# Moving the second half's LayerNorm from the boundary between two token halves into the first half's expert loop

## The reference

```python
mod = (silu(c) @ wmod).reshape(B, 6, 1, D)     # sa, ca, ga, sb, cb, gb
h = layernorm(x) * (1 + ca) + sa
x = x + ga * attn(h)                            # causal attention, then @ wo
h = layernorm(x) * (1 + cb) + sb
# ffn(h):
shared = (silu(h @ Wsg) * (h @ Wsu)) @ Wsd
probs = softmax(h @ W_g); combine = probs kept at its top 2
y_e = (silu(h @ W_gate[e]) * (h @ W_up[e])) @ W_down[e]   # all 8 experts, all tokens
x = x + gb * (shared + sum_e combine[:, e] * y_e)
```

## Time and profile before

| | |
|---|---|
| median of 3 runs | 1937.34 us (1935.97 to 1938.6) |
| profiled execution, its own time | 1932.17 us |
| its span, core 2 (all cores 1918.4 to 1930.2) | 1930.2 us |
| mean granted TensorE clock, core 2 | 0.787 |
| busy: TensorE matmul, VectorE, ScalarE, GpSimd | 67%, 39%, 22%, 11% |
| chain that ended last: TensorE, VectorE, issue, DMA, ScalarE | 57%, 16%, 11%, 8%, 7% |
| first down matmul of expert 0 for tiles 8 to 15 | at 1536.14 us |

### The profile page before, as it was taken

How to read it: one execution, slowest core, us unless ns; L and a number is a source line. 1 busy time by engine, 2 the same in 40 slices (tenths; PEclk the granted TensorE clock), 3 DMA queues, 4 the chain that set the end, 5 groups by cost and what they waited for, 6 DMA issues and landing times.

```text
span 1930.2 us, 20470 instructions; the slowest of 8 cores (1918.4 to 1930.2 us)
## 1 busy us (share of the span) xinstructions
PE 1288.8 (67%) x5238; PEld 487.1 (25%) x5238; DVE 755.2 (39%) x1449; ACT 434.2 (22%) x735; POOL 216.1 (11%) x226
## 2 busy tenths in 40 slices
PE   3713263236767431658979889799914599999998
PEld 0111121110221101222323333243302233333333
DVE  0354534551144515354233323444354433333333
ACT  0030201210046243415434335310132100000010
POOL 0002020033455773000000000000000000000000
PEclk8955556558965655667989899899956799999999
DMA  9605150079987674000111011021210021121225
GB/s 284 165 0 163 46 164 1 25 228 313 287 247 226 212 213 167 1 1 26 63 44 66 23 44 66 22 66 66 66 43 1 22 66 66 66 66 66 67 78 184
DMA packets 90437, 193.99 MB, mean 101 GB/s; under 512 B 14184, under 2 KB 14248, under 8 KB 90328
## 3 DMA queue, kind: packets, MB, share of 16 engines
q1 hardware_dynamic: 64848, 130.64, 22.4%
q10 hardware_dynamic: 16648, 33.60, 5.8%
q0 software_dynamic: 8832, 28.45, 3.7%
HBM read 155.92 MB, written 36.70 MB: 100 GB/s over the span
## 4 chain that ended last, share of the span: by engine, by line
PE 57%; DVE 16%; issue 11%; DMA 8%; ACT 7%; DVEq 1%; ACTq 0%; POOL 0%; SPq 0%; POOLq 0%
PE ps L950 13%; PE ps L917 13%; PE ps L932 12%; DMA stage<-wmod 5%; PE ps L1088 4%; PE ps L552 4%; PE ps L453 3%; PE ps L1031 3%; DVE h1b L545 2%; DVE h1b L542 2%; DVE st_sm L505 2%; DMA q_aug<-bbf 2%; PE ps L706 2%; PE ps L607 1%; ACT pT L1093 1%
## 5 line engine op out<-in xcount | busy, mean ns | idle before, releaser
L950 PE MATMUL ps<-down_bf,act_e 128*128 128x512 bf16 x1152 | 292.2, 392 | 38.2 <-DVE act_e L940 15.4
L917 PE MATMUL ps<-hT,gate_bf 128*128 128x512 bf16 x1152 | 283.4, 391 | 20.5 <-ACT r_t L886 13.7
L932 PE MATMUL ps<-hT,up_bf 128*128 128x512 bf16 x1152 | 274.4, 381 | 2.0 <-ACT r_t L886 0.8
L940 DVE TENSOR_TENSOR act_e<-ps,silu_s 128x512 bf16<-128x512 f32 x144 | 99.6, 691 | 422.9 <-PE ps L932 353.4
L959 DVE SCALAR_TENSOR_TENSOR x_res<-ps,comb,x_res 128x512 f32<-128x512 f32 x256 | 192.1, 750 | 145.4 <-PE ps L950 141.6
L552 PE MATMUL ps<-ident,h1b 128*128 128x128 f32 x256 | 69.2, 425 | 268.7 <-DVE h1b L545 268.7
L926 ACT ACTIVATE silu_s<-ps 128x512 bf16<-128x512 f32 x144 | 86.0, 597 | 554.1 <-PE ps L917 553.9
L1093 ACT ACTIVATE pT<-ps 128x512 bf16<-128x512 f32 (+3 forms) x320 | 158.8, 531 | 140.2 <-PE ps L1088 127.8
L950 PEld LDWEIGHTS ps<-down_bf,act_e 128*128 128x128 bf16 x1152 | 99.8, 99 | 225.3 <-issue 149.3
L917 PEld LDWEIGHTS ps<-hT,gate_bf 128*128 128x128 bf16 x1152 | 112.8, 100 | 167.8 <-issue 45.1
L932 PEld LDWEIGHTS ps<-hT,up_bf 128*128 128x128 bf16 x1152 | 112.9, 98 | 143.1 <-issue 11.2
(11 more groups left out here) (118 smaller groups left out, 842.7 us busy)
## 6 DMA issues: line engine op xcount, KB each, us to landing
stage<-wmod ACTq DMA_DIRECT2D x96, 256.0 KB, 10.3
gate_bf<-wc_g SPq DMA_DIRECT2D x72, 256.0 KB, 4.8
up_bf<-wc_u SPq DMA_DIRECT2D x72, 256.0 KB, 3.4
down_bf<-wc_d SPq DMA_DIRECT2D x72, 256.0 KB, 3.6
pc_in<-w_gate SPq DMA_DIRECT2D x64, 256.0 KB, 6.1
pc_in<-w_up SPq DMA_DIRECT2D x64, 256.0 KB, 4.2
pc_in<-w_down SPq DMA_DIRECT2D x32, 512.0 KB, 4.2
wc_g<-pc_o POOLq DMA_DIRECT2D x36, 256.0 KB, 4.9
```

Source lines behind the costliest of these rows:

```text
L917: tok = P.op("t", lambda e, buf=buf, hc=hc, qc=qc, dc=dc, psg=psg: e.matmul(psg[:, :], gate_bf[:, buf, dc, 128 * hc:128 * (hc + 1)], hT[:, ...
L932: tok = P.op("t", lambda e, hc=hc, qc=qc, dc=dc, psu=psu: e.matmul(psu[:, :], up_bf[:, dc, 128 * hc:128 * (hc + 1)], hT[:, dc, 512 * qc:51 ...
L940: P.op("v", lambda e, hc=hc, qc=qc, ssl=ssl, psu=psu: e.tensor_tensor(act_e[:, hc, 512 * qc:512 * (qc + 1)], psu[:, :], silu_s[:, ssl, :], ...
L950: tok = P.op("t", lambda e, i=i, dch=dch, hc=hc, psd=psd: e.matmul(psd[:, :], act_e[:, hc, 128 * i:128 * (i + 1)], down_bf[:, hc, 512 * dc ...
```

## The change

The LayerNorm of tiles 8 to 15 and its eight routers become a function, `emit_ln2h2`. The loop of the first half's mixture calls it once, as a whole, after the first unit at which the attention steps are through and all eight `attn_out_tile` have been emitted; if that never happened, it is called behind the loop. Its callback has only the routers. Expert 0's gate and up for tiles 8 to 15 are no longer in the callback but are ordinary units of the second half's list (`skip_e0_gateup=False`). `gate_dma(0, ...)` and `up_dma(0)` keep their place behind the loop and now come after the LayerNorm's instructions in the text.

```diff
+        ln2h2_done = [False]
+
+        def emit_ln2h2():
+            ln2h2_done[0] = True
+
+            def _grp_cb1(grp):
+                for i in range(8 + 4 * grp, 8 + 4 * grp + 4):
+                    emit_router(i)
+
+            layernorm_phase(t0=8, ngrp=2, group_cb=_grp_cb1, pstb=(2, 3),
+                            dump=stage[:, 0:2, :].rearrange("p a b -> p (a b)"),
+                            dump_bufs=[b_stage[0], b_stage[1]])
+
         units = moe_unit_list(0, skip_e0_gateup=True)
...
                 _fin2()
                 if ui % 3 == 0:
                     attn_out_tile(ao_left.pop(0))
+            elif st_done >= nst and not ln2h2_done[0]:
+                emit_ln2h2()
...
-        h2buf = _gbuf[0]
-        gate_dma(0, h2buf)
+        if not ln2h2_done[0]:
+            emit_ln2h2()
+        gate_dma(0, _gbuf[0])
         up_dma(0)
-
-        def _grp_cb1(grp):
-            for i in range(8 + 4 * grp, 8 + 4 * grp + 4):
-                emit_router(i)
-            emit_gateup(0, h2buf, 2 + grp)
-
-        layernorm_phase(t0=8, ngrp=2, group_cb=_grp_cb1, pstb=(2, 3),
-                        dump=stage[:, 0:2, :].rearrange("p a b -> p (a b)"),
-                        dump_bufs=[b_stage[0], b_stage[1]])
-        for u in moe_unit_list(1, skip_e0_gateup=True):
+        for u in moe_unit_list(1, skip_e0_gateup=False):
             u()
```

## The result

The changed kernel is **slower by 0.46%**: ratio 1.0046, 95% interval 1.0031 to 1.0061, medians 1945.62 against 1937.13 us over 11 runs each. The forecast was 1944.7 and slower.

A forecast was written before the change was run, and what follows sets the result against it. A VectorE and ScalarE chain was taken to set the pace inside the 134.8 us around the norm, TensorE outside. Terms summed to +7.4 us, 1939.6 by the profiled execution, carried over to 1944.7 us; range 1940.5 to 1950.0.

The forecast's parts named there:

- Where the code lands: The whole LayerNorm with its routers is emitted after expert 7's third down tile, 57.3 us earlier; TensorE's hole moves along.
- (a): Callback of group 0: without gate and up, 26.91 us becomes the router chain's 16.3, -10.6 us.
- (b): Norm of group 1: with no matmuls ahead, its first transposes run slow too, +0.4 us.
- (c): Callback of group 1: 27.81 us becomes 16.1, a router chain less one table load plus 1.0 before tile 4, -11.7 us.
- (d): Expert 7's remaining down tiles 4 to 7: 10.1 us becomes 10.3 with a partly cold start, +0.2 us.
- (e): Expert 0's gate and up for tiles 8 to 15 follow expert 8's last down matmul, 27.8 us warm: +28.4 us.
- (f): SiLU's table load returns in expert 8's first gate block with TensorE waiting: +0.7 us, bounds 0 and 1.3.
- (g): Weight loads keep their order on SP's queue and land under other work: DMA counted at nothing.
- only about 3.3 us are truly overlapped: Callback of group 0: chain and gate-and-up block end to end would be 30.2 us; the callback took 26.9.
- the clock pays: Rival: if TensorE's work set the callbacks' length, saved cold restarts and table loads gain 5.9 us, 1931.4; chance 6%.

The follow-up runs named there:

- e10: Changed kernel plus 24 spare matmuls under the second group's router chain, 16 before down tile 3 and 8 behind it; stretch 199.7 us, ratio 1.0029.
- e6: Changed kernel with the routers of tiles 8 to 15 computed for four tiles at once; stretch 179.0 us (three cores 180.3), ratio 0.9925.
- e3: Kernel before with the eight routers of tiles 8 to 15 left out, their weights a constant; stretch 174.7 us (two cores 175.3), ratio 0.9908.
- e4: Changed kernel with the eight routers of tiles 8 to 15 left out, their weights a constant; stretch 169.6 us (one core 168.7), ratio 0.9866.
- e7: Kernel before plus eight spare matmuls between the fourth router's matmuls and the gate matmuls of both callbacks; stretch 193.6 us, ratio 1.0010.
- e5: Kernel before with the routers of tiles 8 to 15 computed for four tiles at once; stretch 176.0 us (three cores 177.0), ratio 0.9915.
- e8: Kernel before with the norm split by half tiles, pieces put behind gate and up pairs, and short routers; stretch 110.8 us, ratio 0.9577.

## Why the prediction was right, step by step

The direction, the size and the place were right: +7.4 forecast, +8.1 in the stretch, +8.5 between the medians. That the median of whole runs came within 1 us of the 1944.7 is partly luck: the two profiled executions differ by 3.5 us before the stretch begins.

- **Where the code lands.** Right: the first sum follows expert 7's third down tile, at 1347.46 in the kernel after; MoE matmuls nowhere stand between the transposes.
- **(a) Callback 0**: forecast -10.6, measured 16.63 - 26.91 = -10.3; one VectorE instruction of the chain started some 0.4 us late, which accounts for it.
- **(b) Norm 1**: +0.4; measured +0.5, the first transposes at 1.08 us.
- **(c) Callback 1**: -11.7; measured 16.40 - 27.81 = -11.4. The table load was saved as argued: the exponential of router 12 begins 0.25 us after its maximum, that of router 8 1.53 after. The Trainium skill ("ScalarE: Activation LUTs", What ACT_TABLE_LOAD costs) adds 1.38 us of drain to the load; the exponential moved by 1.28, the load alone, on a ScalarE that had been idle before it, so here the trace differs from the page.
- **(d) Tiles 4 to 7**: I chose 2.5 cold groups, +1.7, between bounds of 0 and 5.8. Measured 10.55 us where I had 10.3, and e10 shows 2.0 of it to be the cold restart. The clock was low for the whole of callback 1 (0.50), so tile 3's matmuls, which ran in two lots of four with 2.19 us between, did not raise it. The doubt was real: in e6, where the eight ran without that gap, tiles 4 to 7 had a clock of 1.00 on core 3 and of 0.83 on core 7.
- **(e), (f) Expert 8 and expert 0's gate and up**: forecast +28.4 and +0.7; measured 46.84 + 29.01 - 47.2 = +28.6 together. SiLU's load idled TensorE 0.50 us and made expert 8's gate and up 0.7 longer, as forecast. What I had missed is small: the wait before expert 8's first down matmul fell from 1.75 to 1.40 us, and expert 0's gate followed its last down matmul 0.2 us sooner than that one's modelled end.
- **(g) DMA**: no wait of TensorE on a load appears in the stretch.
- The statistics took 0.3 us more, which I had not foreseen.

One sentence of mine was misleading though its sum was right: "only about 3.3 us are truly overlapped". That was the *net* of each callback. The runs without routers show 13.2 us of chain hidden in the two callbacks together, and 5.1 us that the old grouping paid for it, 3.9 of them in one cold restart and two hand-overs. **The rival "the clock pays"** thus named a real gain (it put it at 5.9; 5.1 is what e3 and e4 leave), but e7 shows that with the chains in place the restart cannot be collected, and the chains are worth more. The Trainium skill's advice to gather matmuls ("TensorE: Matmul & The Clock Gate", Loop structure matters more than you think) agrees with e3 against e4, where nothing stood beside the matmuls (2.1 of the 5.1 us are the clock's), and not with this change, where they covered VectorE's work.

Not settled: the 1.2 us of the -5.1 outside the group boundary were not taken apart, and why the clock comes back later on some cores of e5 and e6 than on others (1.0 to 1.3 us of the stretch) no run shows.

## What to carry to other kernels

Before moving matmuls into a dense, warm stretch, ask what they were covering where they stood: here they were the only cover of a 16 us chain of 0.2 us VectorE instructions, and dense they covered none of it. Moving a serial phase as one block moves the hole with it; what paid here (e8) was to cut it into pieces that fit another engine's idle time (2.8 us of VectorE in each gate and up pair) and to give it banks of its own. And measure such a change between two landmarks in the trace: 0.1 to 0.2 us of repeatability there in most kernels, and 1.3 at worst, against several us in the whole run.

## What the runs showed of the hardware

- A cold restart of TensorE has no fixed price: 0 us under the router chain (e7), 2.0 us in front of down tiles (e10), 2.1 us in front of an uncovered gate and up pair (e3), and 0 or 1.3 us for the same four down tiles on two cores of one execution (e6).
- The routers' VectorE instructions on 128x8 elements cost 0.26 to 0.34 us from start to start, those on 128x4x8 about 0.29 (e5, e6): four times the elements for the same time. That is how a chain of 16.3 us became one of 5.2.
- Neither ScalarE's 64 scalings of h1b nor its 32 squares had a table load before them, behind exponentials, SiLU or the square root: all 37 loads of the kernel before stand before an exponential (16), SiLU (16), the square root (4) or the logarithm (1).
